# An order for one attention step written anew: the last bank of transposed probabilities in the q and k bank, the q and k product behind the scores, the output product in the outputs' bank

## The reference, cut to what matters

```python
h = layernorm(word_emb[ids] + pos_emb + type_emb[types]) * gamma + beta     # 16 sequences x 128 tokens, 256 wide
a = layernorm(h)
q, k, v = a @ Wq, a @ Wk, a @ Wv                  # 16 heads of 16
q, k = layernorm over each head of q, k (with its weight and bias)
p = softmax(causal(q @ k.T / 4))
h = h + (p @ v) @ Wo + bo
x2 = layernorm(h)
scores = softmax(x2 @ gate_w.T)                   # 8 experts, the best two by scores + expert_bias
h = h + sum over the two experts of (silu(xs @ w1) * (xs @ w3)) @ w2, with xs = x2 * score
```

## Time and profile before

| | us |
|---|---|
| median of three runs | 578.4 (576.05 to 580.04) |
| the profiled execution's own time | 577.32 |
| its span in the trace | 575.3 |
| first scores of sequence 0 | 38.7 |
| scores of sequence 15 | 215.7 |
| first expert matmul | 259.9 |

### The profile page before, as it was taken

One profiled execution on the slowest core, in us unless ns is written; L12 is line 12 of the kernel. 1 busy time (PEld: TensorE's weight loads), 2 busy tenths in 40 slices (PEclk: granted clock), 3 DMA queues, 4 the chain that ended last, 5 costly groups with the idle time before them and its releaser, 6 DMA issues.

```text
span 575.3 us, 12790 instructions
## 1 busy us (share of the span) xinstructions
PE 500.3 (87%) x4198; PEld 428.7 (75%) x4199; DVE 290.9 (51%) x705; ACT 255.1 (44%) x591; POOL 283.1 (49%) x540
## 2 busy tenths in 40 slices
PE   6558988889889887348999999999999999999991
PEld 2235666766667665228999999999999999999981
DVE  3657788787787766673333333333333333333330
ACT  1138867888778885005223333222333332233320
POOL 6887677777774221211544444444444444444442
PEclk9889999999999998559999999999999999999996
DMA  5006630110006775100211222221122222212221
GB/s 157 19 11 201 213 114 28 46 36 28 27 27 201 238 239 179 34 13 26 31 30 34 37 37 37 37 36 29 28 37 37 37 37 37 28 28 37 37 37 18
DMA packets 29480, 36.62 MB, mean 64 GB/s; under 512 B 7792, under 2 KB 23024, under 8 KB 29456
## 3 DMA queue, kind: packets, MB, share of 16 engines
q0 software_dynamic: 8352, 12.76, 12.9%
q1 hardware_dynamic: 20288, 22.51, 12.0%
q10 hardware_dynamic: 816, 1.06, 0.6%
HBM read 26.81 MB, written 9.50 MB: 63 GB/s over the span
## 4 chain that ended last, share of the span: by engine, by line
PE 65%; ACT 14%; DVE 8%; POOL 5%; issue 5%; DMA 1%; DVEq 0%; SPq 0%; ACTq 0%; POOLq 0%
PE PS L1168 33%; PE PS L1179 17%; ACT work L534 8%; PE PS L978 5%; PE PS L1053 3%; DVE nmax L764 3%; ACT work L541 2%; PE PS L1020 2%; PE PS L1122 2%; PE PS L1015 1%; ACT w_sb L571 1%; POOL rstd L397 1%; PE PS L986 1%; ACT w_sb L578 1%; ACT x2T L546 1%
## 5 line engine op out<-in xcount | busy, mean ns | idle before, releaser
L1168 PEld LDWEIGHTS PS<-work,arena 128*128 128x128 f32 x1716 | 197.6, 192 | 3.9 <-ACT work L638 2.0
L1168 PE MATMUL PS<-work,arena 128*128 128x128 f32 x1716 | 198.1, 275 | 1.5 <-ACT work L638 1.5
L644 ACT ACTIVATE work<-PS 128x768 f32<-128x768 f32 x39 | 31.6, 810 | 197.1 <-PE PS L1168 197.1
L1179 PE MATMUL PS<-w_sb,work 128*128 x468 | 107.6, 379 | 0.7 <-DVE x_pair L953 0.7
L945 DVE TENSOR_TENSOR work<-work,PS 128x640 f32<-128x640 f32 x39 | 32.0, 821 | 139.5 <-ACT work L644 139.5
L1179 PEld LDWEIGHTS PS<-w_sb,work 128*128 128x128 f32 x468 | 85.9, 190 | 11.2 <-issue 1.1
L534 ACT ACTIVATE work<-PS,nmax 128x128 f32<-128x128 f32 x256 | 76.5, 434 | 36.9 <-DVE nmax L764 36.9
L481 POOL DMA_INDIRECT out_dram<-x_pair,dst_c x39 | 78.7, 2018 | 23.4 <-POOL dst_c L480 21.9
L480 POOL COPY dst_c<-dest_i 128x1 int32 (+1 forms) x39 | 7.1, 182 | 137.4 <-DVE x_pair L953 135.1
L978 PE MATMUL PS<-ident,work 128*128 128x128 f32 x336 | 55.1, 277 | 12.2 <-ACT work L534 12.1
L634 ACT ACTIVATE arena<-w_sb 128x1408 f32 x40 | 55.1, 1377 | 17.8 <-DVE er_i L918 12.8
(11 more groups left out here) (144 smaller groups left out, 625.0 us busy)
## 6 DMA issues: line engine op xcount, KB each, us to landing
w_sb<-w_dram SPq DMA_DIRECT2D x16, 640.0 KB, 6.1
w_sb<-w_dram SPq DMA_DIRECT2D x8, 704.0 KB, 4.6
x_rows<-x SPq DMA_DIRECT2D x16, 128.0 KB, 1.8
out_dram<-arena SPq DMA_DIRECT2D x16, 128.0 KB, 1.8
w_sb<-w_dram SPq DMA_DIRECT2D x16, 64.0 KB, 6.1
w_sb<-w_qkv_dram ACTq DMA_DIRECT2D x1, 768.0 KB
work<-x_rows,src_c POOLq DMA_INDIRECT x41, 2.8
out_dram<-x_pair,dst_c POOLq DMA_INDIRECT x39, 4.1
```

The source lines that it names most:

```text
L1168: last = n.matmul(up_ps[p][:, i, c, :], ws[p][:, k, at:at + P], xT_sb[p][:, k, :], start=(k == 0), stop=(k == DK - 1))
L1179: last = n.matmul(PS[:, 7, 0:D], hT_sb[p][:, i, :], w2_sb[:, bass.ds(e, 1), i, :], start=(i == 0), stop=(i == FK - 1))
```

## The change

It changes no arithmetic, only places and order.

- **Banks.** The fourth bank of transposed probabilities (`keys_to_rows(3)`) goes to `T_BANK` in place of bank 3, and ACT's `transposed(3)` reads it there. The product with Wo goes to the upper half of `O_BANK` in place of `VY_BANK`. The waits follow: the q and k transposes wait until the last sequence's `transposed(3)` is done, `x2_to_rows` and `keys_to_rows(3)` until q and k are copied, the `a_n` transposes until the residual of the sequence before last is done (`var_f`).
- **Masks.** `mask_bank(u, r)` is issued one by one at the end of the step before; that of bank 3 needs only the last exponentials, so scores wait for `transposed(2)` and no more for `transposed(3)`.
- **PE.** After the scores come the `a_n` transposes (of t+2, at the start of the step, not of t+3 at the end of the step before), the q and k transposes of t+1, `outputs(t-1)` and the q and k product for t+2. The product with Wo moves ahead of `keys_to_rows(3)`.
- **ACT.** The `aT` copy comes first in the step, squares and the q and k copies move between the second and the third exponentials, `oT` ahead of the fourth, `transposed(2)` directly behind the fourth.
- **DVE and POOL.** All four maxima come first; the sums of squares follow x2 in the middle of the step, and `qkn` of the same sequence stands near the step's end; `row(u)` of t+4 (L837) is computed ahead of `a_n` of t+3. On POOL, `qk_power` is for t+2 and stands behind the embedding's power; the power for `a_n` follows it and stands ahead of the two additions.
- **Run-in.** In step -1 the 14 matmuls of `keep_warm(WARM_FIRST)` stand behind the q and k product of sequence 1 and ahead of the v product and the masks of sequence 0.

The core of the diff:

```diff
-                    a.activation(probsT[:, r * 512:(r + 1) * 512], PS[:, r, :], ACT.Copy).then_inc(probsT_ready, 1)
+                    a.activation(probsT[:, r * 512:(r + 1) * 512], PS[:, T_BANK if r == RG - 1 else r, :], ACT.Copy).then_inc(probsT_ready, 1)
...
-                    link(v.tensor_tensor(row(u), row(u), PS[:, VY_BANK, D:2 * D], ALU.add))
+                    link(v.tensor_tensor(row(u), row(u), PS[:, O_BANK, D:2 * D], ALU.add))
...
+                def mask_bank(u, r):
+
+                    if not isinstance(u, int) or u > 0:
+                        if r == RG - 1:
+                            pe.wait_ge(exp_done, RG * u)
+                        else:
+                            pe.wait_ge(probsT_ready, RG * (u - 1) + r + 1)
+                    n.matmul(PS[:, r, :], identb[:, :], spread(mask[:, :], 1, GROUPS), start=True, stop=True)
...
+                    if r == RG - 1:
+                        wait(pe, logits_read, t - 1)
+                        wait(pe, qk_ready, t + 2)
+                    transposes(probs[:, r * 512:(r + 1) * 512], GROUPS,
+                               T_BANK if r == RG - 1 else r).then_inc(probsT_ps, 1)
...
-                    wait(pe, qk_ready, u + 3)
+                    wait(pe, qk_ready, u + 4)
...
+                    pe.wait_ge(a_ready, u + 1)
+                    wait(pe, var_f, u - 3)
+                    wait(pe, aT_ready, u)
+                    transposes(a_n, DK, O_BANK).then_inc(aT_ps, 1)
...
+                    pe.wait_ge(qkn_ready, u + 1)
+                    if not edge or t > 0:
+                        pe.wait_ge(probsT_ready, RG * t)
+                    transposes(qkn, 2 * DK, T_BANK).then_inc(qk_ps, 1)
```

More of the change, by code:

```diff
@@ L433, in step @@
                     power(0, rstd_e, link)
+                u = t + 2
+                if valid(u):
+                    qk_power(u, link)
+                u = t + 4
+                if valid(u):
+                    pool.wait_ge(var_a, u + 1)
+                    power(1, rstd_a, link)
                 u = t + 3
@@ L585, in step @@
                     exponentials(1)
+                if valid(t + 2):
+                    squares(t + 2)
+                if valid(t + 1):
+                    queries_and_keys_out(t + 1)
+                if valid(t):
+                    transposed(0)
                 if valid(t - 2):
@@ L588, in step @@
                 if valid(t):
-                    transposed(0)
                     exponentials(2)
                     transposed(1)
+                if valid(t - 1):
+                    normalized_out(t - 1)
+                if valid(t):
                     exponentials(3)
+                    transposed(2)
                 if valid(t + 1):
@@ L806, in step @@
                     choose(2, link)
+                u = t + 4
+                if valid(u):
+                    dve.wait_ge(x_used, u + 1)
+                    dve.wait_ge(rstd_e, u + 1)
+                    link(v.scalar_tensor_tensor(row(u), tmp, rstd[:, 0:1], beta, ALU.mult, ALU.add))
                 u = t - 2
@@ L834, in step @@
                 if valid(u):
-                    dve.wait_ge(x_used, u + 1)
-                    dve.wait_ge(rstd_e, u + 1)
-                    link(v.scalar_tensor_tensor(row(u), tmp, rstd[:, 0:1], beta, ALU.mult, ALU.add))
                     stats(link, row(u), 1, var_a)
@@ L1008, in step @@
                 edge = isinstance(t, int)
+                def mask_bank(u, r):
[5 more added lines that the diff above has]
+                    n.matmul(PS[:, r, :], identb[:, :], spread(mask[:, :], 1, GROUPS), start=True, stop=True)
                 def scores():
-                    for r in range(RG):
-                        if not edge or t > 0:
-                            pe.wait_ge(probsT_ready, RG * (t - 1) + r + 1)
-                        n.matmul(PS[:, r, :], identb[:, :], spread(mask[:, :], 1, GROUPS), start=True, stop=True)
                     pe.wait_ge(qk_ready, t + 1)
@@ L1029, in outputs @@
                     wait(pe, aT_ready, u + 4)
+                    if edge and t + 2 >= B:
+                        wait(pe, var_f, u)
                     wait(pe, oT_ready, u)
@@ L1114, in step @@
                     keys_to_rows(3)
-                u = t - 1
-                if valid(u):
-                    pe.wait_ge(oT_ready, u + 1)
-                    wait(pe, v_ready, u + 3)
-                    wait(pe, var_f, u)
-                    for k in range(DK):
-                        last = n.matmul(PS[:, VY_BANK, D:2 * D], oT[:, k, :], wo_sb[:, k, :],
-                                        start=(k == 0), stop=(k == DK - 1))
-                    last.then_inc(wo_done, 1)
-                u = t + 3
-                if valid(u):
-                    pe.wait_ge(a_ready, u + 1)
-                    wait(pe, oT_ready, t)
-                    wait(pe, aT_ready, u)
-                    transposes(a_n, DK, O_BANK).then_inc(aT_ps, 1)
+                if valid(t + 1):
+                    mask_bank(t + 1, 3)
+                    mask_bank(t + 1, 2)
             pe.wait_ge(pool_const, 2)
```

147 lines of the change are left out of this document (71 added, 76 removed).

## The result

The changed kernel takes 582.97 us in the median of 7 runs (581.74 to 584.13), the kernel before, run beside it on the same chip, 578.15 (576.05 to 580.04): ratio 1.0084, 95% interval 1.0064 to 1.0104. The forecast was 579.0 with a range of 570 to 588, and no change by more than 1%. That holds, but the kernel is a little slower for certain, by some 5 us of the 5.8 that I had called no change, and the loss sits partly where I did not look. The profiled execution has 582.24 and a span of 580.3, against 577.32 and 575.3.

The account below looks back on a forecast made before the run. No engine was full, so a ring of waits (11.85 us) was taken to set the attention step. Run-in +2.7, sequences 0 and 1 -0.7, twelve steps -1.6, sequence 14 +0.1 gave +0.5: 579.0 us forecast, range 570 to 588.

Parts of the forecast that it names:

- The ring through the q and k path: Scores to scores through `a_n` transposes, `aT` copy, `outputs`, product, squares, copies, x2, exponentials, last transposes and masks: sum 11.98.
- Its size: Length of the changed step: 11.85 us, bounds 11.6 and 12.4; 12 steps gain 12 x 0.13 = 1.6 us.
- the deduction of 0.13: On ACT, shorter rows because short waits leave less backlog: 0.13 off the summed step of 11.98.
- two masks at 3.19 / 14 = 0.22: 0.44: On PE at the step's end, two masks ahead of the next scores, priced from the 14 warm-up matmuls: 0.44 us.
- The run-in: Up to the first scores: warm-ups and v product behind the product, less an earlier `qkn`: +2.7 us, bounds +1.0 and +6.
- the -0.9 for `qkn` 0: In the run-in, Newton for sequence 0 starts at 29.0 instead of 29.87: -0.9 us, bounds -2 and +1.5.
- Sequences 0 and 1: First two steps, lacking `outputs` or x2 in the ring: about 10.2 and 11.2, together 21.4, a gain of 0.7 us.
- Sequence 14: Step without a product behind its scores but 9 small rank products ahead of the last transposes: about 11.3, +0.1 us.
- Tail: Last steps: `outputs(15)` late by about 1 us but ready before DVE finishes its next lane rows: 0.
- The waits inside ACT's step vanish: Rival: product, x2 and outputs ready in time, ACT sets a step of 11.1; -9 us, 570; chance 0.22.
- DVE's tail holds the `a_n` transposes: Rival: transposes wait for `var_f`, DVE's last work, past a cover of 0.45; step 12.3, +5.9 us, 585; chance 0.14.
- run-in rival: Warm-ups at the lower clock (over 0.3 each) or `qkn(0)` after 34: +6 instead of +2.7, 586; chance 0.14.

Follow-up runs that it names:

- Experiment 1: Changed kernel with the 14 warm-up matmuls put back to the start of step -1: 584.08 us, ratio 1.0117 to the kernel before.
- 9: Changed kernel with the 14 warm-ups at the start of step -1 and the first maxima ahead of `qkn` of sequence 1: 583.81 us, ratio 1.0090.
- 7: Changed kernel with eight more warm-up matmuls in step -1, behind the `a_n` transposes of sequence 1: 581.68 us, ratio 1.0069.
- experiment 6: Changed kernel with q and k copies ahead of squares, x2 transposes ahead of v product, output division ahead of sums of squares, residual ahead of `qkn`: 574.13 us.
- 8: Changed kernel with the moves of experiment 6 and the eight more warm-up matmuls of 7: 573.66 us, ratio 0.9915.
- experiment 3: Changed kernel with ACT's q and k copies ahead of the squares and PE's x2 transposes ahead of the v product: 587.06 us, ratio 1.0152.

## Why the prediction came out as it did

The time was inside the range, but its parts were not what the sum had. It said +0.5 us, and the span grew by 5.0. Of the 4.5 missed, 3.8 lie in the twelve steps, 0.7 in the run-in, 0.5 in sequences 0 and 1, and -0.5 behind them. The steps have the wrong sign: a gain of 1.6 was forecast, a loss of 2.2 measured, and their 12.16 lies just outside the 11.6 to 12.1 that the chance of 0.50 was given for. That "within 1%" still came true is owed to the width of that 1%, 5.8 us, and so in part to luck.

*The ring through the q and k path*: right, and within 0.15 us at every mark up to the start of exponentials 3 (9.81 behind the scores, 9.78 summed). From the scores (137.14) the `a_n` transposes load 1.10 later as forecast, ACT's copy follows at 1.58 (1.60), the squares at 5.24 (5.10), the x2 copy at 7.80 (7.79), exponentials 2 at 8.08 (8.05). ACT waits 0.27 ahead of the squares (0.25) and 0.29 ahead of the raw outputs (0.25), with the wait ahead of the `aT` copy 1.87 in all, where about 2.4 was expected.

*Its size*: 11.85 forecast, 12.16 measured. Two steps of the prediction failed. The first is the comparison: 11.85 is the length of one ring, set against 11.98, a mean of twelve steps in the kernel before, although its own ring was 11.85 as well. Its steps in the loop were 11.84 to 11.91 in turn with 12.26 to 12.43, and the forecast put this share at nothing for the changed kernel. Like against like, the forecast held no gain at all, and 0.09 of each step's miss is here: 12.08 in turn with 12.31. In the kernel before, a long step loses the time between scores and first maximum, 1.69 (144.90 to 146.59) instead of 1.28:

```profile
146.59 1.29 DVE L764 TENSOR_REDUCE nmax<-PS 128x4 f32<-128x512 f32 x2 [0.42 <-PE PS L1020]
```

In the changed kernel it comes in three parts. In the step from 149.21 the `a_n` transposes load 1.11 behind the scores, as in the step before, but ACT's `aT` copy starts 0.08 later (1.66 instead of 1.58), the squares are 0.16 later (154.61) and the x2 copy 0.24 (157.25), and that stays to the step's end:

```profile
150.87 0.38 ACT L584 ACTIVATE front<-PS 128x256 f32<-128x256 f32 x1 [1.38 <-PE PS L982]
```

I have no row that names the cause of any of the three.

The second is the ring's own length, 12.07 in the step from 137.14 against 11.98 before the deduction of 0.13. The deduction was real (the q and k copies took 1.47 and not 1.66, exponentials 3 ended 0.07 sooner), but small terms ate it: the product was ready 0.14 later than summed, the last transposes took 0.05 more, and the mis-sized term is "two masks at 3.19 / 14 = 0.22: 0.44". From the first mask's matmul to the scores' loads are 0.52. The masks,

```profile
148.58 0.21 PEld L1021 LDWEIGHTS PS<-mask,identb 128*128 128x128 bf16 x2
148.69 0.59 PE L1021 MATMUL PS<-mask,identb 128*128 128x512 bf16 x2
```

the last of them by itself,

```profile
148.91 0.38 PE L1021 MATMUL PS<-mask,identb 128*128 128x512 bf16 x1
```

and the last one of the kernel before, with scores at 144.90:

```profile
144.59 0.38 PE L1015 MATMUL PS<-mask,identb 128*128 128x512 bf16 x1
```

The second mask follows the first by 0.22, as counted, but the scores' loads follow the start of the last mask by 0.30 (149.21), not by 0.22. It was 0.31 in the kernel before, hidden in the 0.51 of its ring, so the trace of before had the price.

Two lesser slips, which moved nothing: 11.85 - 0.76 is 11.1 and not 11.2 for sequence 1, and the times of the rivals (570, 585, 586) are counted from 579.0, which holds the forecast's own +0.5, and not from 578.4.

*The run-in*: +2.7 forecast, +3.39 measured at the loads of the first scores. As the sum of what stands ahead of that point it was nearly right: from `qkn` 0 to the loads +3.65 were forecast, +3.74 measured (9.27 against 5.53). The mis-sized term is the -0.9 for `qkn` 0, which came at 32.80 against 33.15: -0.35. `a_n` of sequence 0 came at 21.02 ("about 20.5"). What failed is the reason for the cost, "In the changed order warm-up and v product stand behind the product: +3.0 + 0.87". They do, but beside a longer chain: `qkn` 0 (32.80), product (34.46, 2.93), squares (37.43), Newton (39.25 to 42.98), `qkn` 1 (43.02), maxima (43.62). From `qkn` 0 to the maxima are 10.8 us. In the kernel before, `qkn` 1 stood behind the first maxima, and the product of sequence 2 that follows it only at 45.27, beside exponentials and transposes. Experiment 1 shows that the warm-ups cost nothing there and in fact keep the clock up for the product that follows, 9 that earlier maxima win nothing while the product of sequence 2 stands where it does, and 7 that a shorter product shortens the chain.

*Sequences 0 and 1*: -0.7 forecast, -0.2 measured. *Sequence 14*: +0.1, measured -0.1. *Tail*: 0, measured -0.3; between variants with the same tail it ranges over 1.4 us (357.86 in experiment 6, 359.2 in 8), so a third of a microsecond there says nothing.

*The rivals.* "The waits inside ACT's step vanish" needed an open ring, and even with both rings open the step was 11.5, not 11.1. "DVE's tail holds the `a_n` transposes" is not what the changed kernel does, but it was near: a delay of the squares by 1.3 (experiment 3) brought it in. The cover that the prediction put at 0.45 was 0.78 in the changed kernel (statistics done at 149.54, transposes at 150.32). Of the run-in rival neither sign came: the 14 warm-ups took 3.19, at the full clock, and `qkn` 0 stood at 32.80, not after 34. What ran at the lower clock in part was the product ahead of them (2.93 against 1.98 in a step), as the same product did in the kernel before (2.87).

*GpSimd beside VectorE.* `row(u)` (L829, L837 before) is the instruction for which I feared 0.88 or more beside POOL. Its durations in the changed kernel (min, median, max in ns, first and last start), in five middle steps,

```profile
L829 DVE SCALAR_TENSOR_TENSOR arena<-front,rstd,rows_sb x5: 525/526/549, 108.8 to 157.5; 128x256 f32 x5
```

and in the kernel before:

```profile
L837 DVE SCALAR_TENSOR_TENSOR arena<-front,rstd,rows_sb x4: 766/882/892, 118.1 to 154.0; 128x256 f32 x4
```

It became 0.36 shorter: it now stands beside Newton's operations of 32 columns (145.28 beside L406 and L407) and no longer beside POOL's addition of 256 columns. The Trainium skill ("GPSIMD Engine Reference", "Specifications") has the two engines share SBUF interfaces, with contention when a DVE instruction has two SBUF inputs. That agrees, but I had its sign wrong here: the 0.4 each that I allowed for two instructions was, for this one, a gain of 0.36. That POOL's narrower operations are the cause is read from rows side by side; no experiment moved them alone.

## What to carry to other kernels

A step's length is the longest of several rings, so write down the second longest before moving work: here one of 12.16 hid one that became 12.46 as soon as the first was opened, each part of the cure alone gained nothing or lost, and all together gained 0.6 a step. In a run-in, follow the chain of dependences of the next item too; filler that looks like the delay may lie beside it, and here it was also what kept PE's clock up. Set a ring against a ring and a mean against a mean, or the share of the loop turns up as a gain. Read idle time ahead of a weight load beside the row of its matmuls: "issue" there can be a wait for another engine.

## What the hardware showed that I had not expected

- ACT's durations went with what stood ahead of them: 512 columns took 0.60 behind an idle time, 0.80 at the end of an unbroken row; the three q and k copies 1.47 and 1.66.
- Adding eight matmuls to a waiting PE ahead of a product shortened that product from 2.93 to 1.97 and the run-in by 0.56 (3.15 to 2.19 and 0.10 in experiments 6 and 8).
- The scores' weights loaded 0.30 and 0.31 behind the start of the last mask's matmul in both kernels, though these matmuls follow one another by 0.22 and no engine is named in the wait.
- Steps of a loop unrolled by two differed in turn, by 0.4 to 0.6 in the kernel before and by 0.24 in the changed one.
- `row(u)` on DVE took 0.88 beside POOL's wide operations and 0.53 beside its narrow ones.
